# A bidirectional state-space layer on one core: gates by tanh without a clamp on POOL, softplus products two steps apart, five slots for the dt diagonals, first inputs in halves

## Chip, core and metric

The kernel runs on one core of a Trainium2 chip. The metric is the time of one execution on the device in microseconds (us). Engines go by their short names: PE is TensorE, DVE is VectorE, ACT is ScalarE, POOL is GpSimd, SP is SyncE (here it only starts DMAs). Each engine works through its own queue in order; a wait for a semaphore stops that engine's whole queue.

## What is computed

For 16 sequences of 256 tokens with 256 channels, in float32, a conditioned layer is computed: normalise and modulate, run a selective state-space model forward and backward, add, then a gated two-layer perceptron. Cut to the part that the change touches:

```python
xs, z = split(h @ in_w, 2)                   # 512 channels each
xs = silu(xs)
proj = xs @ xproj_w                          # dt, B, C
dt = softplus(proj[..., :512] + dt_bias)
hst = hst * exp(dt * A) + (dt * xs) * B      # 64 states per channel, one token after the other
y = sum(hst * C) + xs * Dskip
return y * silu(z) @ out_w                   # also backward over the tokens
```

Silu is x * sigmoid(x). Softplus is log(1 + exp(v)).

## The kernel before, in words

`main_phase` does everything up to `y`; `output_phase` does the rest and isn't touched. `main_phase` is unrolled completely. It makes 16 passes: 8 pairs of sequences (`CB = 2`), each in two directions. A pass is 128 steps (`JP`), and a step is one scan on DVE (`scan`, L889): a 128 x 1024 `tensor_tensor_scan` over 32 tokens of a part of the states. 16 steps are a chunk of 32 tokens, so a pass has 8 chunks, numbered from 0. Two steps are a pair; POOL's loop runs over the 64 pairs of a pass.

One step needs from the others:

- PE (`step`): for step j it injects the inputs into the bank `u[j % 2]` (`inject`, L1031, 4 matmuls in 2 parts), computes the exponents of step j + 2 (`exponent`, L1044), and adds up outputs of earlier steps (`add_up`, L1063). It may start step j when scan j - 2 has ended, since `u` has two slots.
- ACT (`one_pass`): `put_carry` (L816) writes the carried state of step j into bank `u`, then `decay` (L797, L798) takes the exponentials for step j + 2, and every eighth step `read_y` (L809) empties the output bank.
- POOL (`one_pass`, pair i): `turn_dt` (L535) makes the diagonal tile `dd` for pair i + 2, `turn_u` (L544) makes `ud` for pair i + 1, `carry_in` (L570 and L575) makes the carried state of steps 2i and 2i + 1, from chunk 1 on. `spread_c` (L557) comes once a chunk in its third pair, `first_inputs` (L563) once a chunk in its seventh pair, for the chunk that follows.
- The scan of step j waits for the inject, for `decay` and, from chunk 1 on, for `put_carry`; every eighth one also for an `add_up`.

Beside this, each pass carries the preparation of the following pass, a "unit", cut into small pieces. Each engine has a generator `unit(q)`; PE and ACT take one piece after each step (slot j), POOL takes two per pair from its third pair on, one between `carry_in(2i)` and `turn_u(i + 1)`, one after `carry_in(2i + 1)`. So piece k of POOL lies beside step k + 4. The slots of a unit: 16 projections of x and z, one each third slot from 0 to 45 (`project_xz`, L942, 4 recorded matmuls each); 8 half-projections of dt and 2 of B and C, each over two slots, from 48, 51, 54, 57, 60, 63, 72, 75, 84 and 87 on (`project`, L950); transposes at 66, 69, 78, 90 and 98. With an odd q the next pair of sequences is also normalised (`variance`, `root`, `normalise`) and turned (slots 108 and 112); DVE then takes its statistics between scans 64 and 78. The last pass has no unit. The unit of pass 0 runs before the first scan, without anything beside it.

Before, a gate takes: `take_xz` (L658) copies the projection out of PSUM in two halves; POOL clamps it from below (L473); ACT makes exp, log of 1 + that, and exp again (L642, L645, L648), one slot apart; POOL multiplies (L479). A softplus of a 128-channel block takes: Relu and Abs out of PSUM on ACT (L668, L669), exp, 1 + exp, log and minus 1 (L675 to L682, semaphore `logged`), then four products or sums on POOL (`softplus`, L485, L488, L492, L497) in four pieces one after the other, then 8 free pieces.

All of exp, log, Copy, Relu, Abs and Identity are in the one table set that ACT loads at the start (L613). Three PSUM banks, `e`, are handed out in `share_banks` to exponents and to the unit's matmuls; PE waits before a bank for whoever reads it last.

`dd` and `ud` have four slots each (`NPR`), so `turn_dt` of pair i + 2 waits until scan 2i - 3 has ended:

```python
pool.wait_ge(scanned, scanned_to(p, 2 * (i - NPR) + 1))
```

Of the kernel before, what the change touches and what calls it, by code (L numbers as in the profile page):

```python
# [58 lines left out]
def main_phase(nc, x, cond, w_mod, b_mod, w_in, w_xp, dt_bias, a_log, mod, scr):  # L59
# [4 lines left out]
    with ctx:  # L64
# [9 lines left out]
        NDA, NPR, NM, NDT = 4, 4, 4, 3  # L74
# [17 lines left out]
        dd = sb("b_dd", [P, NPR, TT, TC])  # L92
# [19 lines left out]
        cl = sb("b_cl", [P, 2, T])  # L112
# [65 lines left out]
        chain = sem("b_chain")  # L178
# [22 lines left out]
        UT_SLOT = (66, 78, 90, 98)  # L201
        BC_SLOT, BT_SLOT = 54, 69
        TURN_SLOT = (108, 112)
# [78 lines left out]
        with nc.Block() as block:  # L282
# [163 lines left out]
            def _(pool):  # L446
# [20 lines left out]
                def clamp(q, i):  # L467
                    m = q * SILUS + i
                    src = xs[:, i, :] if i < JB else sd[:, i - JB, :]
                    pool.wait_ge(freed, first_job(q) + CB * i + CB)  # L470
                    if m >= 2:
                        pool.wait_ge(silu_made, m - 1)
                    nc.gpsimd.tensor_scalar(cl[:, i % 2, :], src, CLAMP, None, ALU.max).then_inc(clamped, 1)  # L473

                def times_sigmoid(q, i):
                    m = q * SILUS + i
                    dst = xs[:, i, :] if i < JB else sd[:, i - JB, :]
                    pool.wait_ge(chain, 3 * m + 3)
                    nc.gpsimd.tensor_tensor(dst, dst, cl[:, i % 2, :], ALU.mult).then_inc(silu_made, 1)  # L479

                def softplus(q, j):
# [11 lines left out]
                    yield  # L493
# [4 lines left out]
                    yield  # L498

                def unit(q):  # L500
                    for i in range(SILUS):
                        clamp(q, i)
# [27 lines left out]
                def turn_dt(p, i):  # L530
# [3 lines left out]
                    pool.wait_ge(scanned, scanned_to(p, 2 * (i - NPR) + 1))  # L534
                    nc.gpsimd.tensor_tensor(dd[:, i % NPR, :, :], dr[:, c % 2, v:v + 1, :].broadcast_to((P, TT, TC)),  # L535
# [24 lines left out]
                def first_inputs(p, c):  # L560
                    pool.wait_ge(f_loaded[c % 2], loaded_to(p, c, F_DMAS))
                    flat = u0[:, c % 2, :, :, :].rearrange("p k v d -> p (k v d)")
                    nc.gpsimd.tensor_tensor(flat, flat, b0[:, c % 2, :].broadcast_to((P, DI)), ALU.mult).then_inc(u0_made, 1)  # L563
                    pool.wait_ge(u0_made, p * (NCH - 1) + c)
# [19 lines left out]
                def one_pass(p, last, side):  # L584
                    for i in range(PAIRS):
# [9 lines left out]
                        if v == STEPS // 2 - 2 and c + 1 < NCH:  # L595
                            first_inputs(p, c + 1)
# [12 lines left out]
            def _(act):  # L609
# [27 lines left out]
                def sigmoid(q, i):  # L637

                    m = q * SILUS + i
                    both = cl[:, i % 2, :]  # L640
                    act.wait_ge(clamped, m + 1)
                    nc.scalar.activation(both, both, ACT.Exp, scale=-1.0).then_inc(chain, 1)  # L642
                    yield
                    act.wait_ge(chain, 3 * m + 1)
                    nc.scalar.activation(both, both, ACT.Ln, bias=1.0).then_inc(chain, 1)  # L645
                    yield
                    act.wait_ge(chain, 3 * m + 2)
                    nc.scalar.activation(both, both, ACT.Exp, scale=-1.0).then_inc(chain, 1)  # L648

                def take_xz(q, i, b):  # L650
                    n = first_job(q) + CB * i + b
                    act.wait_ge(full, n + 1)
# [5 lines left out]
                    nc.scalar.activation(dst[:, b * SEQ:(b + 1) * SEQ], job_bank(n)[:, 0:SEQ], ACT.Copy).then_inc(freed, 1)  # L658
# [52 lines left out]
                def unit(q):  # L711
                    for i in range(SILUS):
# [812 lines left out]
```

## Time and profile before

| | us |
|---|---|
| median of 3 runs | 5516.26 (5516.01 to 5521.09) |
| the profiled execution | 5517.54 |
| its span, first to last instruction | 5515.8 |
| mean granted PE clock | 0.974 |
| busy: PE, DVE, ACT, POOL | 5024.7, 4741.2, 3408.5, 3910.0 |
| DVE's scans (2048) | 4554.2 |
| first scan starts, last scan of the last pass ends | 118.9, 5057.9 |

The rows further down are of four kinds. The page's busy line and groups of instructions give totals. Windows give a stretch (from:to and its length), how much of it PE, the weight load PEld, DVE, ACT and POOL were busy (with the number of instructions), the granted PE clock as a share of full speed, the DMA share and GB/s. The timeline lists instructions in order of time: start, length, engine, line, operation, tiles, and in square brackets how long the engine sat idle and who ended it. Adjacent instructions of one engine overlap a little in the records: two scans that follow one another without a wait start 2.18 us apart, though one is recorded as 2.29 us. So a shown idle time of x stands for a delay of about x + 0.11. Rows of equal instructions without a wait between them are merged (x3).

### The profile page before, as it was taken

The page shows a single profiled execution, that of the slowest core. Times are in us where ns is not written, and L with a number is a line of the kernel's source. Part 1 is how long each engine was busy: PE and PEld are TensorE (multiplying, and loading weights), DVE is VectorE, ACT ScalarE, POOL GpSimd, SP SyncE. Part 2 cuts the span into 40 slices and gives each one's busy share as a digit, 9 for nine tenths or more (in the row PEclk, how much of TensorE's full clock was granted, in tenths as well). Part 3 has the DMA queues.
Part 4 walks back from the last instruction along what each step waited for, and adds up shares of the span by engine and source line. Part 5 has one row for each costly group of instructions (what it writes and reads, how often), then busy time and mean ns, then how long its engine had stood idle before and what let it go on. Part 6 is the DMA issues. An engine that isn't in the chain of part 4 may idle for free. (4 is left out here: it accounts for less than half of the span.)

```text
span 5515.8 us, 130520 instructions
## 1 busy us (share of the span) xinstructions
PE 5024.7 (91%) x44784; PEld 2544.5 (46%) x44784; DVE 4741.2 (86%) x2419; ACT 3408.5 (62%) x11450; POOL 3910.0 (71%) x6629
## 2 busy tenths in 40 slices
PE   5999989898999989898999989898999989886898
PEld 4444444444444444444544444444444444443444
DVE  1989898989989898989989898989989898997443
ACT  4766666666766666666766666666766666564111
POOL 4877777787877777787877777787877777674111
PEclk8999999999999999999999999999999999998999
DMA  3111111111111111111111111111111111112552
GB/s 101 50 49 49 56 34 61 42 50 48 52 50 49 54 36 60 42 51 48 51 50 49 54 36 57 45 52 48 51 50 44 53 37 45 35 29 82 156 156 65
DMA packets 433144, 306.75 MB, mean 56 GB/s; under 512 B 215920, under 2 KB 336240, under 8 KB 432496
## 3 DMA queue, kind: packets, MB, share of 16 engines
q1 hardware_dynamic: 428272, 294.39, 17.8%
q8 instruction: 349, 5.72, 0.4%
q10 hardware_dynamic: 4224, 4.19, 0.2%
q14 instruction: 299, 2.45, 0.1%
HBM read 187.27 MB, written 111.15 MB: 54 GB/s over the span
## 5 line engine op out<-in xcount | busy, mean ns | idle before, releaser
L889 DVE TENSOR_TENSOR_SCAN b_hs<-b_dA,b_u 128x1024 f32<-128x1024 f32 x2048 | 4554.2, 2272 | 394.0 <-ACT b_u L816 309.8
L1044 PE MATMUL b_ex<-b_dd,b_aw 32*128 32x512 f32 x8192 | 2794.6, 651 | 59.0 <-ACT b_dA L798 31.3
L1031 PE MATMUL b_u<-b_ud,b_bw 32*128 32x256 f32 x16384 | 2364.3, 405 | 314.0 <-DVE b_hs L889 305.3
L798 ACT ACTIVATE b_dA<-b_ex 128x496 f32<-128x496 f32 x4096 | 2290.5, 589 | 180.6 <-PE b_ex L1044 178.4
L1031 PEld LDWEIGHTS b_u<-b_ud,b_bw 32*128 32x128 f32 x16384 | 1456.0, 187 | 1200.7 <-issue 719.6
L535 POOL TENSOR_TENSOR b_dd<-b_dr,b_mask 128x512 f32<-128x512 f32 x1024 | 1072.5, 1047 | 567.2 <-DVE b_hs L889 546.6
L1063 PE MATMUL b_y<-b_hs,b_cw 128*32 128x256 f32 x16384 | 1329.7, 396 | 2.3 <-DVE b_hs L889 2.3
L816 ACT ACTIVATE b_u<-b_hin 128x32 f32<-128x32 f32 x1792 | 364.9, 204 | 1361.9 <-PE b_u L1031 868.2
L544 POOL TENSOR_TENSOR b_ud<-b_ur,b_mask 128x512 f32<-128x512 f32 x1024 | 1082.3, 1057 | 0.0
L1044 PEld LDWEIGHTS b_ex<-b_dd,b_aw 32*128 32x128 f32 x8192 | 874.6, 186 | 109.4 <-ACT b_dA L798 70.0
L1063 PEld LDWEIGHTS b_y<-b_hs,b_cw 128*32 128x32 f32 x16384 | 326.5, 109 | 1055.9 <-issue 1055.3
L797 ACT ACTIVATE b_first<-b_ex 128x16 f32<-128x16 f32 x3584 | 644.1, 180 | 13.0 <-PE b_ex L1044 7.3
L575 POOL TENSOR_TENSOR b_hin<-b_hm,b_u 128x32 f32<-128x32 f32 x1792 | 450.8, 252 | 140.4
L570 POOL TENSOR_TENSOR b_hm<-b_first,b_hs 128x32 f32<-128x32 f32 x1792 | 480.3, 268 | 94.2 <-ACT b_first L797 85.7
L950 PE MATMUL b_ex<-b_xs,b_wxp 128*128 128x256 f32 x1256 | 353.8, 405 | 0.7 <-ACT b_ey L669 0.7
L1199 POOL TENSOR_TENSOR c_gs<-c_gs,c_sz 128x512 f32<-128x512 f32 x64 | 79.0, 1274 | 302.1 <-DVE c_gs L1405 302.1
L942 PE MATMUL b_ex<-b_hT,b_win 128*128 128x256 f32 x1008 | 288.2, 410 | 5.3 <-ACT b_hT L628 3.1
L950 PEld LDWEIGHTS b_ex<-b_xs,b_wxp 128*128 128x128 f32 x1256 | 214.7, 190 | 142.4 <-issue 99.2
L942 PEld LDWEIGHTS b_ex<-b_hT,b_win 128*128 128x128 f32 x1008 | 174.4, 192 | 120.8 <-issue 96.9
L485 POOL TENSOR_TENSOR b_nd<-b_wy,b_ey 128x512 f32<-128x512 f32 x64 | 81.4, 1272 | 183.3 <-ACT b_wy L682 183.3
L473 POOL TENSOR_SCALAR b_cl<-b_xs 128x512 f32<-128x512 f32 x64 | 95.0, 1485 | 124.0 <-ACT b_xs L658 124.0
L473 POOL TENSOR_SCALAR b_cl<-b_sd 128x512 f32<-128x512 f32 x64 | 95.0, 1484 | 82.1 <-ACT b_sd L658 82.1
(106 smaller groups left out, 2491.2 us busy)
## 6 DMA issues: line engine op xcount, KB each, us to landing
b_u<-scratch_ut SPq DMA_DIRECT2D x256, 128.0 KB, 2.9
scratch_y<-b_ysb SPq DMA_DIRECT2D x128, 256.0 KB, 2.3
scratch_xs<-b_xs SPq DMA_DIRECT2D x64, 256.0 KB, 2.1
scratch_sz<-b_sd SPq DMA_DIRECT2D x64, 256.0 KB, 2.2
scratch_dt<-b_sd SPq DMA_DIRECT2D x64, 256.0 KB, 2.2
scratch_ut<-b_uT SPq DMA_DIRECT2D x64, 256.0 KB, 2.3
b_ur<-scratch_ut SPq DMA_DIRECT2D x1024, 16.0 KB
b_dr<-scratch_dt SPq DMA_DIRECT2D x1024, 16.0 KB, 1.7
```

The costliest lines, as they stand in the source:

```text
L535: nc.gpsimd.tensor_tensor(dd[:, i % NPR, :, :], dr[:, c % 2, v:v + 1, :].broadcast_to((P, TT, TC)), mask[:, :].unsqueeze(2).broadcast_to(( ...
L544: nc.gpsimd.tensor_tensor(ud[:, i % NPR, :, :, :], ur[:, c % 2, :, v * TT:(v + 1) * TT].unsqueeze(3).broadcast_to(shape), mask[:, :].unsqu ...
L570: nc.gpsimd.tensor_tensor(hm[:, j % NM, :, :].rearrange("p h d -> p (h d)"), e0[:, j % NM, :, :].rearrange("p h d -> p (h d)"), hs[:, v, : ...
L575: nc.gpsimd.tensor_tensor(hin[:, j % NM, :, :], hm[:, j % NM, :, :], u0[:, c % 2, 2 * kp:2 * kp + 2, v, :], ALU.add).then_inc(hin_made, 1)
L797: nc.scalar.activation(e0[:, j % NM, h, :], src[:, :, 0], ACT.Exp).then_inc(e0_done, 1)
L798: nc.scalar.activation(dA[:, j % NDA, h, :, 1:TC], src[:, :, 1:TC], ACT.Exp).then_inc(exp_done, 1)
L889: nc.vector.tensor_tensor_scan(hs[:, v, :, :, kp].rearrange("p d t -> p (d t)"), dA[:, j % NDA, :, :, :].rearrange("p h d t -> p (h d t)") ...
L942: last = nc.tensor.matmul(job_bank(n)[:, 0:SEQ], win[:, k, i * P:(i + 1) * P], hT[:, q % DIRS, k, b * SEQ:(b + 1) * SEQ], start=(k == 0), ...
L950: ins = nc.tensor.matmul(job_bank(n)[:, 0:SEQ], wxp[:, k, cols], xs[:, k, b * SEQ:(b + 1) * SEQ], start=(k == 0), stop=(k == JB - 1))
L1031: ins = nc.tensor.matmul(dst[:, :, tb, :], bw[row(r), c % 2, tb, :], ud[row(r), j // 2 % NPR, tb, :, :], start=(tb == 0), stop=(tb == NTB ...
L1044: nc.tensor.matmul(e[bank_of[what]][:, :], aw[row(r), p % DIRS, v, :, :].rearrange("p b s -> p (b s)"), dd[row(r), j // 2 % NPR, :, :].rea ...
L1063: ins = nc.tensor.matmul(y[q * QR:(q + 1) * QR, cols], cw[:, n, q, g * QR:(g + 1) * QR], hs[:, f * (SPN // 2):(f + 1) * (SPN // 2), :, q * ...
```

## The change

- A gate becomes x/2 * (1 + tanh(x/2)). `take_xz` reads PSUM twice, once with Copy and scale 0.5, once with Tanh and scale 0.5 into `th`; `plus_one` adds 1 on ACT one slot after the second half; POOL multiplies as before. The clamp on POOL and the three functions on ACT are gone. Before Tanh, ACT waits until POOL's product of two gates earlier is done (`silu_made`).
- Tanh is in another table set. Each unit loads `exp_and_others` at its start and `natural_log_exp_and_others` after the gates (slot 48).
- The four pieces of `softplus` on POOL stand two pieces apart, with 4 free pieces behind them and not 8. What hangs on the last of them moves: the fourth transpose from slot 98 to 101, ACT's root from 101 to 103, the turning from 108 and 112 to 110 and 114.
- `dd` has five slots, with a running index over passes, so `turn_dt` of pair i + 2 waits for scan 2i - 5.
- `first_inputs` is done in two halves, in the sixth and the seventh pair of a chunk.

```diff
-        NDA, NPR, NM, NDT = 4, 4, 4, 3
+        NDA, NPR, NDD, NM, NDT = 4, 4, 5, 4, 3
...
-        UT_SLOT = (66, 78, 90, 98)
+        UT_SLOT = (66, 78, 90, 101)
         BC_SLOT, BT_SLOT = 54, 69
-        TURN_SLOT = (108, 112)
+        TURN_SLOT = (110, 114)
...
-                def clamp(q, i):
-                    m = q * SILUS + i
-                    src = xs[:, i, :] if i < JB else sd[:, i - JB, :]
-                    pool.wait_ge(freed, first_job(q) + CB * i + CB)
-                    if m >= 2:
-                        pool.wait_ge(silu_made, m - 1)
-                    nc.gpsimd.tensor_scalar(cl[:, i % 2, :], src, CLAMP, None, ALU.max).then_inc(clamped, 1)
-
                 def times_sigmoid(q, i):
...
-                    pool.wait_ge(chain, 3 * m + 3)
-                    nc.gpsimd.tensor_tensor(dst, dst, cl[:, i % 2, :], ALU.mult).then_inc(silu_made, 1)
+                    pool.wait_ge(raised, m + 1)
+                    nc.gpsimd.tensor_tensor(dst, dst, th[:, i % 2, :], ALU.mult).then_inc(silu_made, 1)
...
                     nc.gpsimd.tensor_tensor(nd[:, :], wy[:, :], ey[:, :], ALU.subtract).then_inc(nd_made, 1)
-                    yield
+                    yield from wait_steps(2)
...
                 def unit(q):
                     for i in range(SILUS):
-                        clamp(q, i)
                         yield from wait_steps(2)
...
                         yield from softplus(q, j)
                         if j < JB - 1:
-                            yield from wait_steps(8)
+                            yield from wait_steps(4)
                     if q % DIRS and q + 1 < PASSES:
                         c = q // DIRS + 1
-                        yield from wait_steps(2)
                         variance(c)
...
-                    pool.wait_ge(scanned, scanned_to(p, 2 * (i - NPR) + 1))
-                    nc.gpsimd.tensor_tensor(dd[:, i % NPR, :, :], dr[:, c % 2, v:v + 1, :].broadcast_to((P, TT, TC)),
+                    pool.wait_ge(scanned, scanned_to(p, 2 * (i - NDD) + 1))
+                    nc.gpsimd.tensor_tensor(dd[:, (p * PAIRS + i) % NDD, :, :], dr[:, c % 2, v:v + 1, :].broadcast_to((P, TT, TC)),
...
-                def first_inputs(p, c):
+                def first_inputs(p, c, k):
                     pool.wait_ge(f_loaded[c % 2], loaded_to(p, c, F_DMAS))
...
+                    some = u0[:, c % 2, 2 * k:2 * k + 2, :, :].rearrange("p k v d -> p (k v d)")
+                    nc.gpsimd.tensor_tensor(some, some, b0[:, c % 2, :].broadcast_to((P, DI // 2)), ALU.mult).then_inc(u0_made, 1)
+                    if k:
+                        pool.wait_ge(u0_made, 2 * (p * (NCH - 1) + c))
...
-                        if v == STEPS // 2 - 2 and c + 1 < NCH:
-                            first_inputs(p, c + 1)
+                        if v in (STEPS // 2 - 3, STEPS // 2 - 2) and c + 1 < NCH:
+                            first_inputs(p, c + 1, v - (STEPS // 2 - 3))
...
-                    nc.scalar.activation(dst[:, b * SEQ:(b + 1) * SEQ], job_bank(n)[:, 0:SEQ], ACT.Copy).then_inc(freed, 1)
+                    nc.scalar.activation(dst[:, cols], job_bank(n)[:, 0:SEQ], ACT.Copy, scale=0.5)
+                    if m >= 2:
+                        act.wait_ge(silu_made, m - 1)
+                    nc.scalar.activation(th[:, i % 2, cols], job_bank(n)[:, 0:SEQ], ACT.Tanh, scale=0.5).then_inc(freed, 1)
+
+                def plus_one(q, i):
+                    act.wait_ge(freed, first_job(q) + CB * i + CB)
+                    nc.scalar.activation(th[:, i % 2, :], th[:, i % 2, :], ACT.Identity, bias=1.0).then_inc(raised, 1)
...
                 def unit(q):
+                    nc.scalar.preload_act_table_set("exp_and_others")
                     for i in range(SILUS):
                         take_xz(q, i, 0)
...
                         take_xz(q, i, 1)
                         yield
-                        next(last, None)
-                        yield
-                        yield
-                    last = sigmoid(q, SILUS - 1)
-                    next(last)
+                        plus_one(q, i)
+                        yield from wait_steps(2)
+                    nc.scalar.preload_act_table_set("natural_log_exp_and_others")
```

## Rows read from the trace of the kernel before

**Rows 1.** The page, part 1: busy us (share of the span) xinstructions.

```profile
PE 5024.7 (91%) x44784; PEld 2544.5 (46%) x44784; DVE 4741.2 (86%) x2419; ACT 3408.5 (62%) x11450; POOL 3910.0 (71%) x6629
```

**Rows 2.** Windows: pass 4, steps 0-47, 48-97, 98-127; last pass, steps 0-47.

```profile
1363.68:1474.17 110.49, 106.02 (x1025) 53.74 (x1025) 106.52 (x50) 78.43 (x249) 88.41 (x137) 1.00 0.16 49
1474.17:1605.84 131.67, 126.72 (x1099) 63.94 (x1099) 114.26 (x58) 86.39 (x305) 102.28 (x181) 0.97 0.19 55
1605.84:1675.67 69.83, 60.01 (x614) 28.89 (x613) 65.98 (x32) 45.00 (x163) 50.98 (x95) 1.00 0.12 33
4779.00:4883.53 104.53, 83.89 (x960) 42.77 (x960) 104.53 (x49) 61.58 (x210) 69.99 (x125) 1.00 0.11 28
```

**Rows 3.** Waits, whole span: who waited for whom, us in total, times, longest.

```profile
POOL b_dd L535 <- DVE b_hs L889: 546.6, 441, 7.2
POOL b_nd L485 <- ACT b_wy L682: 183.3, 64, 3.8
```

**Rows 4.** Timeline of POOL, pass 4, steps 56 to 58: the first softplus.

```profile
1494.57 1.27 POOL L485 TENSOR_TENSOR b_nd<-b_wy,b_ey 128x512 f32<-128x512 f32 x1 [3.63 <-ACT b_wy L682]
1495.80 1.05 POOL L544 TENSOR_TENSOR b_ud<-b_ur,b_mask 128x512 f32<-128x512 f32 x1
1496.82 0.26 POOL L570 TENSOR_TENSOR b_hm<-b_first,b_hs 128x32 f32<-128x32 f32 x1
...
1497.37 1.27 POOL L488 TENSOR_TENSOR b_nd<-b_ln,b_nd 128x512 f32<-128x512 f32 x1
```

**Rows 5.** Timeline of DVE, pass 4: scans 49, 56, 57, 81, 89, 93 and 96.

```profile
1476.68 2.29 DVE L889 TENSOR_TENSOR_SCAN b_hs<-b_dA,b_u 128x1024 f32<-128x1024 f32 x1 [0.23 <-ACT b_u L816]
...
1494.74 2.29 DVE L889 TENSOR_TENSOR_SCAN b_hs<-b_dA,b_u 128x1024 f32<-128x1024 f32 x1 [0.63 <-PE b_y L1063]
1497.77 2.29 DVE L889 TENSOR_TENSOR_SCAN b_hs<-b_dA,b_u 128x1024 f32<-128x1024 f32 x1 [0.75 <-ACT b_u L816]
...
1560.42 2.29 DVE L889 TENSOR_TENSOR_SCAN b_hs<-b_dA,b_u 128x1024 f32<-128x1024 f32 x1 [0.77 <-ACT b_u L816]
...
1581.75 9.00 DVE L889 TENSOR_TENSOR_SCAN b_hs<-b_dA,b_u 128x1024 f32<-128x1024 f32 x4 [0.23 <-ACT b_u L816]
1592.63 2.29 DVE L889 TENSOR_TENSOR_SCAN b_hs<-b_dA,b_u 128x1024 f32<-128x1024 f32 x1 [1.89 <-ACT b_u L816]
...
1601.46 6.64 DVE L889 TENSOR_TENSOR_SCAN b_hs<-b_dA,b_u 128x1024 f32<-128x1024 f32 x3 [0.76 <-PE b_y L1063]
```

**Rows 6.** Timeline of PE, pass 4: step 49's inject, its half-projection, step 50's inject.

```profile
1475.01 0.48 PE L1031 MATMUL b_u<-b_ud,b_bw 32*128 32x256 f32 x2
...
1476.67 1.13 PE L950 MATMUL b_ex<-b_xs,b_wxp 128*128 128x256 f32 x4
1477.73 0.48 PE L1031 MATMUL b_u<-b_ud,b_bw 32*128 32x256 f32 x2
```

**Rows 7.** Timelines of POOL and DVE, pass 4, steps 28 and 29: a clamp, then all first inputs.

```profile
1425.57 1.49 POOL L473 TENSOR_SCALAR b_cl<-b_sd 128x512 f32<-128x512 f32 x1 [1.60 <-ACT b_sd L658]
...
1428.03 1.04 POOL L563 TENSOR_TENSOR b_u<-b_u,b_b 128x512 f32<-128x512 f32 x1
...
1430.11 4.46 DVE L889 TENSOR_TENSOR_SCAN b_hs<-b_dA,b_u 128x1024 f32<-128x1024 f32 x2 [1.16 <-ACT b_u L816]
```

**Rows 8.** Groups by line: busy us, mean ns of one | idle before.

```profile
L563 POOL TENSOR_TENSOR b_u<-b_u,b_b 128x512 f32<-128x512 f32 x112 | 116.5, 1040 | 0.0
L1345 ACT ACT_TABLE_LOAD x8 | 10.3, 1283 | 0.1
```

**Rows 9.** Timeline of ACT, pass 4, step 48 into step 49.

```profile
1474.77 0.67 ACT L642 ACTIVATE b_cl<-b_cl 128x512 f32<-128x512 f32 x1
1476.35 0.20 ACT L816 ACTIVATE b_u<-b_hin 128x32 f32<-128x32 f32 x1 [0.91 <-PE b_u L1031]
```

**Rows 10.** Timeline of POOL before the first scan: two clamps, one gate apart.

```profile
44.69 1.48 POOL L473 TENSOR_SCALAR b_cl<-b_xs 128x512 f32<-128x512 f32 x1 [0.45 <-ACT b_xs L658]
47.86 1.48 POOL L473 TENSOR_SCALAR b_cl<-b_sd 128x512 f32<-128x512 f32 x1 [0.45 <-ACT b_sd L658]
```

More of the change, by code:

```diff
@@ L492, in softplus @@
                     nc.gpsimd.tensor_tensor(sd[:, j, :], pre[:, :], nd[:, :], ALU.add).then_inc(dt_made, 1)
-                    yield
+                    yield from wait_steps(2)
                     pool.wait_ge(dt_made, m + 1)
@@ L497, in softplus @@
                     nc.gpsimd.tensor_tensor(us[:, j % 2, :], sd[:, j, :], xs[:, j, :], ALU.mult).then_inc(u_made, 1)
-                    yield
+                    yield from wait_steps(2)
                 def unit(q):
                     for i in range(SILUS):
-                        clamp(q, i)
                         yield from wait_steps(2)
@@ L635, in modulate, with take_xz @@
                     yield
-                def sigmoid(q, i):
+                def take_xz(q, i, b):
                     m = q * SILUS + i
[L640 to L650, printed above, removed]
                     n = first_job(q) + CB * i + b
+                    cols = slice(b * SEQ, (b + 1) * SEQ)
                     act.wait_ge(full, n + 1)
@@ L711, in unit @@
                 def unit(q):
+                    nc.scalar.preload_act_table_set("exp_and_others")
                     for i in range(SILUS):
                         take_xz(q, i, 0)
-                        last = sigmoid(q, i - 1) if i else wait_steps(2)
-                        yield
-                        next(last, None)
-                        yield
-                        next(last, None)
-                        yield
+                        yield from wait_steps(3)
                         take_xz(q, i, 1)
                         yield
-                        next(last, None)
-                        yield
-                        yield
-                    last = sigmoid(q, SILUS - 1)
-                    next(last)
+                        plus_one(q, i)
+                        yield from wait_steps(2)
+                    nc.scalar.preload_act_table_set("natural_log_exp_and_others")
                     for j in range(JB):
@@ L729, in unit @@
                         take_dt(q, j, 0)
-                        next(last, None)
-                        yield
-                        yield
-                        next(last, None)
-                        yield
+                        yield from wait_steps(3)
                         take_dt(q, j, 1)
@@ L763, in unit @@
                             next(logs, None)
-                            yield from wait_steps(7)
+                            yield from wait_steps(10)
                     take_ut(q, 3)
@@ L767, in unit @@
                         c = q // DIRS + 1
-                        yield from wait_steps(3)
+                        yield from wait_steps(2)
                         root(c)
@@ L1006, in unit @@
                             turn_inputs(q, 2)
-                            yield from wait_steps(8)
+                            yield from wait_steps(11)
                     turn_inputs(q, 3)
                     if q % DIRS and q + 1 < PASSES:
-                        yield from wait_steps(10)
+                        yield from wait_steps(9)
                         for k in range(MB):
@@ L1044, in exponent @@
                     nc.tensor.matmul(e[bank_of[what]][:, :], aw[row(r), p % DIRS, v, :, :].rearrange("p b s -> p (b s)"),
-                                     dd[row(r), j // 2 % NPR, :, :].rearrange("p d t -> p (d t)"),
+                                     dd[row(r), (p * PAIRS + j // 2) % NDD, :, :].rearrange("p d t -> p (d t)"),
                                      start=True, stop=True, tile_position=(r * QR, 0), skip_group_check=True
```

9 lines of the change are left out of this document (3 added, 6 removed).

## The prediction

> **What bounds the kernel now.** I read the busy line first [rows 1]. PE is at 91% and DVE at 86%, so neither is simply the bound, and POOL at 71% looks harmless. The windows say more [rows 2]. In the last pass, which carries no unit, 48 scans take 104.53 us, 2.178 us each, DVE has no gap, and PE is busy for 80% of it: that is the floor of the main phase. In pass 4 the same 48 steps take 110.49 us, 5.96 more; these are the steps with the gates. The next 50 steps, with softplus, take 131.67 us against 50 x 2.178 = 108.9, 22.8 more. The last 30 take 69.83 against 65.3, 4.5 more. So a pass with a unit pays some 33 us for it, with an odd q; about 30 without normalising. Over 15 passes that is nearly 480 us, all that this change can touch, apart from the time before the first scan.
>
> Who makes DVE late? For softplus the POOL timeline shows it [rows 4]. POOL waits 3.63 us for the log. Then it makes the first product (next start 1.23 later), and only then `ud` (1.02) and the carried state (0.55), which scan 57 needs; it starts late by 0.75 + 0.11 = 0.86 [rows 5]. From then on POOL is behind, and each step has one softplus piece, one diagonal tile and one carry: 1497.37 - 1494.57 = 2.80 us against 2.18 of a scan. So each of the next three steps is 0.62 late too. POOL idles 183.3 us in all before such a first product and 546.6 us before `dd` [rows 3], yet delays DVE: its work comes in bursts.
>
> PE is the second cause. A half-projection makes its step 1477.73 - 1475.01 = 2.72 us [rows 6], 0.54 over a scan, and there are two in a row. The stretch from scan 48 (1474.17, where the window of rows 2 starts) to scan 56 (1494.74, rows 5) holds three such doubles and no softplus piece on POOL: 20.57 us for 8 scans, 3.15 over, so 1.05 per double. The change doesn't touch this. A single projection costs 2.72 + 1.67 (from inject to scan, rows 5 and 6) - 2 x 2.178 = 0.03, plus about 0.15 of hand-over: 0.2.
>
> **The gates (steps 0 to 47).** The clamp of 1.49 leaves POOL, 8 per pass. Its place was bad: it waits for ACT (1.60), stands before `ud` and the carry, and in step 28 first inputs of 1.04 follow it, so scan 29 is 1.16 + 0.11 late [rows 7]. What is left for POOL is one product of 1.24 in 6 steps beside 2 x 1.57 per pair, 4.4 us in the fullest pair against 4.36. I take POOL's part as gone. What is late next is PE: ten single projections of 0.2, and at steps 16 and 40, where the scan also waits for an output sum behind a projection, 0.4 each (an estimate: the hand-over again, and scan 56 waits 0.63 for such a sum, rows 5): 2.9 with step 8. So 5.96 - 2.9 = **3.0 us per pass**. Ends: 1.5 (PE takes back what POOL gives) and 4.
>
> On ACT a gate loses three functions on 512 columns (0.67, rows 9) and gains two more halves and one function on 512. Tanh has no row here; I bound it by a third and by three times that 0.67, and take the same length as Exp, since all functions in the groups differ little. Net ACT has less to do, 0.5 us per gate, and at step 49 no log stands before the next carry any more: I count 0.3 us per pass. The new wait before Tanh stands in front of `put_carry` and `decay`. POOL's product of two gates earlier comes right after carry(6i), ACT's Tanh at the end of step 6i behind a projection, about 1.5 us after that carry is needed; the product takes 1.24. Cost nothing; if the cover goes, see the rivals.
>
> **Two table loads per pass.** A load is recorded as 1.283 us [rows 8]. The first falls in chunk 0, where ACT has no carry to write and decays two steps ahead: nothing. The second stands at step 48 in place of an exp that starts at 1474.77; ACT would be done at 1476.05, and it waits until 1476.35 for PE anyway [rows 9]. Nothing again; ends 0 and the whole 2.6 us per pass.
>
> The Trainium skill (ScalarE: Activation LUTs, What ACT_TABLE_LOAD costs) speaks against this: a switch costs the load and a drain of about 1.38 us, 2.66 in all. No row here shows a drain. By that rule the load at step 48 would end 1.1 us after PE released the carry, and the sum would be some 16 us worse over 15 passes.
>
> **Softplus two pieces apart (steps 48 to 97).** All four pieces now lie in one half of each pair, so a step with a piece (2.80) alternates with one without (1.57): 4.37 for two scans, 4.36. POOL no longer falls further behind, but it doesn't catch up either, and the first product still waits for the log and stands before the carry. So the first delay stays each time (57, 69, 81, 93), as does PE's part.
> - Scans 48 to 56: 3.15 stays.
> - From 56 to 81: 1560.42 - 1494.74 = 65.68, 11.2 over 25 scans' 54.45 [rows 5]. Left over: first delays 0.86 + 0.75 + 0.88, DVE's own statistics 0.7, four doubles of PE at 1.05 (the fifth is covered by the delay of 57), and 0.8 since halves of the first inputs meet pieces of softplus in pairs 29 and 30. That is 8.2, a gain of 3.0.
> - From 81 to 89: 21.33, 3.9 over. Two doubles of 1.05 stay: gain 1.8.
> - From 89 to 96: 19.71, 4.5 over. Scan 93 waits 1.89, because first product, `ud` and all first inputs (1.04) stand before its carry. With half of these it is some 0.4 better. Behind it, from 93 to 96, three scans take 8.83, 2.3 over: in this stretch the granted clock is 0.97 on average [rows 2], so for about 131.67 x 0.03 x 2 = 8 us PE ran at 1.2 GHz instead of 2.4, after it had stood behind that same late carry. I assume that it still falls, and take 1.05 for the stretch; if it doesn't, 1.3 more.
>
> Together 5.9; ends 3.5 (each delay that POOL gives up shows up as one of PE) and 12 (the first delays go too).
>
> **Five slots** let `dd` start a pair earlier, so more of the 546.6 us of waiting [rows 3] can be spent ahead. But `carry_in` follows in the same queue and waits for ACT's decay, and before each burst POOL idles already for the log. I count nothing; ends 0 and 2 us per pass. **Halved first inputs**: 1.04 [rows 8] becomes twice something between 0.52 and 1.04, counted above. They need their DMA 2 steps sooner; it has never been waited for (0.0, rows 8). SP's queue for chunk 7 moves back by up to 2 steps, behind the dt store; ends 0 and one scan per pass. **Shifted slots**: the dt store, the fourth transpose and the turning move by 2 or 3 of 128 slots with room behind them; the normalising now meets a half of first inputs: 0.3 us in 7 passes, a loss of 2.
>
> **Before the first scan** nothing covers the gates. They are 47.86 - 44.69 = 3.17 us apart [rows 10], 8 of them; POOL's clamp hands to three functions of ACT. Without it PE is the slowest, two projections of 1.06 (rows 6) each, 2.1. So 8 x 1.05 = **8.4 us**; ends 5 and 11.
>
> **The sum.** 15 x (3.0 + 5.9 + 0.3) = 138, minus 2, plus 8.4: 144.4. The profiled execution (5517.54) stands 1.3 over the median, so I take the difference from the median: 5516.3 - 144 = **5372 us**.
>
> **The rivals.**
> 1. *PE takes it back.* Each delay of POOL today gives PE time in which its doubles go unseen. For: the doubles lie on the same steps as the softplus pieces. By the lower ends, 15 x (1.5 + 3.5) + 5 = 80: about **5436**. Against: the stretch 81 to 89 has 0.62 late scans where no double stands. Chance 0.17.
> 2. *Only PE is left.* With a slot more and no clamp POOL gets ahead of the bursts, and the clock no longer falls. 15 x (4 + 12) + 11 = 251: about **5265**; halfway there, 5310. Against: the first product waits for ACT, not for POOL. Chance 0.15.
> 3. *The table switch costs more than its record.* The trace has no instruction hard behind a load, so it can hold ACT beyond 1.283 us. It decides from 1.58 on (1476.35 - 1474.77); with as much again, 1.283, it is 1.0 x 15 = 15 us: **5387**. Chance 0.15.
> 4. *Slower.* ACT stands before Tanh for POOL's product, and ACT's own decays, which POOL's next carry needs, stand behind it: a circle. It decides from where POOL reaches carry(6i) later than ACT's step 6i. Then each gate costs up to product and carry, 1.24 + 0.55, on DVE: 8 x 1.8 x 15 = 215 us, less the 144: about **5590**. Against: POOL has lost work just there and idled 1.6 us before the clamp. Chance 0.04.
> 5. *The main phase doesn't move*, since POOL's delays are all replaced: only the start gains, **5508**. Chance 0.03.
>
> The forecast has 0.46. From 5300 to 5440 lie the forecast, rival 3 and most of rivals 1 and 2. A measurement of this kernel can tell about 0.2% (11 us) from no change: faster 0.93, same 0.02, slower 0.05.
>
> **What would show it.** Right: no delay of 0.62 in scans 58 to 60, 70 to 72, 82 to 84; scan 29 on time; delays at 57, 69 and 81 as before, 93 near 1.5; doubles still 1.05; first scan at 110.5; ACT idle after the load at step 48. Wrong: ACT waiting for POOL before Tanh, low clock in new places, waits before the first halves, or doubles above 1.05.

## Result, and the profile after

The changed kernel takes 5384.93 us (median of 4 runs, 5378.22 to 5390.21); the kernel before, measured beside it, 5518.24. The ratio is 0.9757, with a 95% interval of 0.9741 to 0.9774: 133 us less, where 144 were forecast. The profiled execution took 5380.16 (span 5378.4, mean granted PE clock 0.981), 137.4 less in span than the one of before.

The page's busy line of after, to hold against [rows 1]:

```profile
PE 4902.5 (91%) x44784; PEld 2509.1 (47%) x44784; DVE 4725.0 (88%) x2419; ACT 3391.5 (63%) x11482; POOL 3758.3 (70%) x6613
```

It looks like the one before. POOL lost 152 us of work and ACT 17, yet PE, which runs as many instructions as before, shows 122 us less too. A part of it is the clock: in the main phase the granted clock stood at half for 160 us before and for 101 after, which makes up some 30 of the 122. The rest is not explained here. The windows of pass 4 (steps 0 to 47, 48 to 97, 98 to 127, with columns as in [rows 2]) say where it went:

```profile
1322.45:1430.33 107.88, 104.23 (x1025) 54.07 (x1025) 105.99 (x49) 76.86 (x251) 77.77 (x134) 1.00 0.16 50
1430.33:1556.01 125.68, 119.86 (x1096) 61.02 (x1095) 113.67 (x60) 86.80 (x305) 99.10 (x176) 0.99 0.19 57
1556.01:1627.69 71.68, 61.12 (x613) 29.32 (x614) 66.11 (x31) 45.21 (x163) 55.06 (x103) 0.98 0.13 35
```

The gates take 2.6 us less, softplus 6.0 less, and the end of the pass 1.9 **more**. One pass is a sample. So here is a table of my own over all passes, from the ends of the 2048 scans: for each stretch, how much longer its scans took than 2.178 us each, per pass, as means over 7 passes with normalising (numbers 0, 2, to 12) and 7 without (1, 3, to 13).

| steps | before, with / without | after, with / without |
|---|---|---|
| 0-47 | 6.25 / 6.40 | 3.82 / 3.65 |
| 48-56 | 3.30 / 3.29 | 3.08 / 3.12 |
| 57-80 | 10.39 / 10.98 | 9.28 / 8.45 |
| 81-88 | 4.49 / 4.53 | 2.64 / 2.65 |
| 89-96 | 4.82 / 5.13 | 3.38 / 2.70 |
| 97-127 | 4.45 / 0.02 | 5.64 / 0.03 |
| sum | 33.7 / 30.4 | 27.8 / 20.6 |

First scan at 108.9 us against 118.9; main phase (first scan to last scan's end) 4820.1 against 4939.0; the rest, code that the change doesn't touch, 449.4 against 458.0. So 10.0 + 118.9 = 128.9 of the 137.4 lie where the change is, and 8.6 in the output phase, which varied from 449 to 461 between the kernels of this study and belongs to no edit.

**The first softplus**, pass 4, on POOL, as in [rows 4]:

```profile
1450.64 1.27 POOL L477 TENSOR_TENSOR b_nd<-b_wy,b_ey 128x512 f32<-128x512 f32 x1 [4.66 <-ACT b_wy L669]
1451.87 1.07 POOL L534 TENSOR_TENSOR b_ud<-b_ur,b_mask 128x512 f32<-128x512 f32 x1
1452.88 0.27 POOL L561 TENSOR_TENSOR b_hm<-b_first,b_hs 128x32 f32<-128x32 f32 x1
1453.24 0.25 POOL L566 TENSOR_TENSOR b_hin<-b_hm,b_u 128x32 f32<-128x32 f32 x1
1453.44 1.05 POOL L525 TENSOR_TENSOR b_dd<-b_dr,b_mask 128x512 f32<-128x512 f32 x1
...
1455.00 1.28 POOL L480 TENSOR_TENSOR b_nd<-b_ln,b_nd 128x512 f32<-128x512 f32 x1
```

After the carry for step 57 `dd` follows at once, and the second product starts only 3.1 us after the first has ended (1.5 before). DVE in pass 4 from scan 56 on, then scans 81 and 93 and the end of the pass, as in [rows 5]:

```profile
1450.81 2.29 DVE L866 TENSOR_TENSOR_SCAN b_hs<-b_dA,b_u 128x1024 f32<-128x1024 f32 x1 [0.62 <-PE b_y L1040]
1453.85 4.46 DVE L866 TENSOR_TENSOR_SCAN b_hs<-b_dA,b_u 128x1024 f32<-128x1024 f32 x2 [0.75 <-ACT b_u L793]
1459.25 4.46 DVE L866 TENSOR_TENSOR_SCAN b_hs<-b_dA,b_u 128x1024 f32<-128x1024 f32 x2 [0.93 <-ACT b_u L793]
...
1514.90 8.86 DVE L866 TENSOR_TENSOR_SCAN b_hs<-b_dA,b_u 128x1024 f32<-128x1024 f32 x4 [0.78 <-ACT b_u L793]
...
1544.89 28.63 DVE L866 TENSOR_TENSOR_SCAN b_hs<-b_dA,b_u 128x1024 f32<-128x1024 f32 x13 [1.47 <-ACT b_u L793]
1573.91 2.29 DVE L866 TENSOR_TENSOR_SCAN b_hs<-b_dA,b_u 128x1024 f32<-128x1024 f32 x1 [0.40 <-ACT b_u L793]
1577.63 11.34 DVE L866 TENSOR_TENSOR_SCAN b_hs<-b_dA,b_u 128x1024 f32<-128x1024 f32 x5 [1.43 <-ACT b_u L793]
1591.20 9.00 DVE L866 TENSOR_TENSOR_SCAN b_hs<-b_dA,b_u 128x1024 f32<-128x1024 f32 x4 [2.23 <-PE b_y L1040]
1601.53 28.42 DVE L866 TENSOR_TENSOR_SCAN b_hs<-b_dA,b_u 128x1024 f32<-128x1024 f32 x13 [1.33 <-ACT b_u L793]
```

Scan 57 still waits 0.75, scan 58 now follows without a wait, 60 too. Scan 59 waits 0.93: it is a double of PE, which the delay of 57 used to hide in part. In the last lines scans 107, 112 and 116 wait 1.43, 2.23 and 1.33; in the kernel before the same stretch had two such waits, 1.14 and 1.32.

**The table load** at slot 48 on ACT, and scan 49:

```profile
1430.91 0.47 ACT L786 ACTIVATE b_ysb<-b_y 128x128 f32<-128x128 f32 x2
1431.40 1.28 ACT L707 ACT_TABLE_LOAD   x1
1432.69 0.20 ACT L793 ACTIVATE b_u<-b_hin 128x32 f32<-128x32 f32 x1
```

```profile
1433.03 2.29 DVE L866 TENSOR_TENSOR_SCAN b_hs<-b_dA,b_u 128x1024 f32<-128x1024 f32 x1 [0.43 <-ACT b_u L793]
```

The load starts 1.07 us after scan 48 does (1430.33), behind `read_y`; the exp of before started 0.60 after it. It ends 2.36 after it, and before ACT wrote this carry 2.18 after it [rows 2, 9]. So scan 49 is 0.2 later than before. The carry starts at the end of the load's record: no drain shows. From a load's start to ACT's next instruction it is 1.29 us in 31 of the 32 loads of units; behind the very first one, before the first scan, ACT also waits 0.93 us for PE.

### The profile page after: what moved, and what is told of

It is laid out like the page before. It is cut to its first block and busy times, and to the rows that moved or that the text cites. A ratio compares the mean times of both kernels' runs of the same rounds, so it can differ in the third digit from the quotient of the medians.

```text
span 5378.4 us, 130410 instructions
## 1 busy us (share of the span) xinstructions
PE 4902.5 (91%) x44784; PEld 2509.1 (47%) x44784; DVE 4725.0 (88%) x2419; ACT 3391.5 (63%) x11482; POOL 3758.3 (70%) x6613
## 5 line engine op out<-in xcount | busy, mean ns | idle before, releaser
L1021 PE MATMUL b_ex<-b_dd,b_aw 32*128 32x512 f32 x8192 | 2688.8, 648 | 50.2 <-ACT b_dA L775 21.8
L525 POOL TENSOR_TENSOR b_dd<-b_dr,b_mask 128x512 f32<-128x512 f32 x1024 | 1074.9, 1050 | 224.5 <-DVE b_hs L866 209.6
L561 POOL TENSOR_TENSOR b_hm<-b_first,b_hs 128x32 f32<-128x32 f32 x1792 | 483.6, 270 | 573.7 <-ACT b_first L774 550.7
L1021 PEld LDWEIGHTS b_ex<-b_dd,b_aw 32*128 32x128 f32 x8192 | 834.9, 185 | 90.5 <-ACT b_dA L775 52.9
L553 POOL TENSOR_TENSOR b_u<-b_u,b_b 128x256 f32<-128x256 f32 x224 | 138.0, 616 | 7.5 <-DMA b_u<-scratch_ut 7.2
L786 ACT ACTIVATE b_ysb<-b_y 128x128 f32<-128x128 f32 x512 | 119.8, 305 | 6.3 <-PE b_y L1040 6.3
```

What stands on the lines that cost most here:

```text
L525: nc.gpsimd.tensor_tensor(dd[:, (p * PAIRS + i) % NDD, :, :], dr[:, c % 2, v:v + 1, :].broadcast_to((P, TT, TC)), mask[:, :].unsqueeze(2). ...
L561: nc.gpsimd.tensor_tensor(hm[:, j % NM, :, :].rearrange("p h d -> p (h d)"), e0[:, j % NM, :, :].rearrange("p h d -> p (h d)"), hs[:, v, : ...
L1021: nc.tensor.matmul(e[bank_of[what]][:, :], aw[row(r), p % DIRS, v, :, :].rearrange("p b s -> p (b s)"), dd[row(r), (p * PAIRS + j // 2) % ...
```

## Experiments

Each kernel is the changed one with one edit. Ratios are to the kernel before, on the same chip. "Undone" means that part as it was before.

### The spacing of softplus undone

```diff
-                    yield from wait_steps(2)
+                    yield
...
-                            yield from wait_steps(4)
+                            yield from wait_steps(8)
```

(The first edit stands behind each of the four pieces; the normalising keeps its place.)

> The changed kernel with the four softplus pieces of POOL in a row again (8 free pieces behind them); all else as changed. Theory of the prediction: each block's second to fourth piece makes a scan 0.62 us late again, three per block, four blocks, less what PE's doubles hide: some 5 us per pass, 75 us in all, about 5460 us, with delays near 0.6 at scans 58 to 60, 70 to 72, 82 to 84. Rival (PE takes it back): PE's doubles lie on the same steps, so under 2 us per pass, below 5415 us.

Measured: 5474.28 us, ratio 0.9915 (0.9898 to 0.9931), 89 us over the changed kernel. Main phase 4909.2. DVE, scans 57 to 60 of pass 4:

```profile
1476.86 2.29 DVE L867 TENSOR_TENSOR_SCAN b_hs<-b_dA,b_u 128x1024 f32<-128x1024 f32 x1 [0.74 <-ACT b_u L794]
1479.64 2.29 DVE L867 TENSOR_TENSOR_SCAN b_hs<-b_dA,b_u 128x1024 f32<-128x1024 f32 x1 [0.50 <-ACT b_u L794]
1483.02 2.29 DVE L867 TENSOR_TENSOR_SCAN b_hs<-b_dA,b_u 128x1024 f32<-128x1024 f32 x1 [1.08 <-ACT b_u L794]
1485.80 4.54 DVE L867 TENSOR_TENSOR_SCAN b_hs<-b_dA,b_u 128x1024 f32<-128x1024 f32 x2 [0.50 <-ACT b_u L794]
```

The row of late scans is back (0.50 + 0.11, the 0.62 of before; at scan 59 a double of PE comes on top). By the table's measure a pass loses 5.5 (with) to 6.4 us (without normalising). PE does not take the gain back.

### The gates undone

```diff
-                    nc.scalar.activation(th[:, i % 2, cols], job_bank(n)[:, 0:SEQ], ACT.Tanh, scale=0.5).then_inc(freed, 1)
...
+                    nc.gpsimd.tensor_scalar(cl[:, i % 2, :], src, CLAMP, None, ALU.max).then_inc(clamped, 1)
```

(The other lines of the gates, table loads included, are reversed with them.)

> The changed kernel with the gates of before (clamp on POOL, three functions on ACT, one table set); all else as changed. Theory of the prediction: 3.3 us per pass (50 us) and about 10 us before the first scan: about 5445 us; the first scan starts near 119 us again and scan 29 is late. Rival (with a fifth slot and halved first inputs POOL hides the clamp by itself): only the start is lost, about 5395 us.

Measured: 5437.77 us, ratio 0.9853 (0.9836 to 0.9869), 53 us over the changed kernel, where 60 were expected. First scan at 119.1; steps 16 to 47 pay 5.5 us per pass against 3.15 to 3.3. Steps 0 to 47 as a whole pay 2.0 to 2.1 more than in the changed kernel, not the 2.4 to 2.8 that the table shows between before and after. With the clamp and the first inputs in halves, scans 29 and 31 are late by 0.85 and 0.49 (passes without normalising), in the kernel before by 1.27 and 0.94. So beside a clamp the halves seem to be worth something; without it, in these steps, whole first inputs cost nothing (below). In the changed kernel the products of two gates before the first scan are 1.76 us apart, on POOL:

```profile
42.19 1.27 POOL L471 TENSOR_TENSOR b_xs<-b_xs,b_th 128x512 f32<-128x512 f32 x1 [0.49 <-ACT b_th L645]
43.95 1.27 POOL L471 TENSOR_TENSOR b_sd<-b_sd,b_th 128x512 f32<-128x512 f32 x1 [0.48 <-ACT b_th L645]
```

It was 3.17 in [rows 10]. This product waits for ACT's "plus one".

### Four slots for dd

```diff
-        NDA, NPR, NDD, NM, NDT = 4, 4, 5, 4, 3
+        NDA, NPR, NDD, NM, NDT = 4, 4, 4, 4, 3
```

> The changed kernel with four slots for dd; all else as changed. Theory of the prediction: the slot is worth nothing by itself, since POOL idles for the log before each burst anyway: within 10 us of the changed kernel, 5380 to 5395 us. Rival (the slot lets POOL get ahead of its bursts, so it carries part of the gain): 2 us per pass, about 5415 us.

Measured: 5385.62 us, ratio 0.9758 (0.9742 to 0.9774): the fifth slot is worth nothing. POOL's waits (us in total, times, longest), of after and then of this kernel, show why:

```profile
POOL b_hm L561 <- ACT b_first L774: 550.7, 711, 3.3
POOL b_dd L525 <- DVE b_hs L866: 209.6, 111, 3.6
```

```profile
POOL b_dd L525 <- DVE b_hs L866: 779.7, 649, 6.8
POOL b_hm L561 <- ACT b_first L774: 74.5, 112, 1.7
```

With a slot more, POOL spends its idle time one instruction later, before the carry, for ACT.

### First inputs in one piece

```diff
-                        if v in (STEPS // 2 - 3, STEPS // 2 - 2) and c + 1 < NCH:
-                            first_inputs(p, c + 1, v - (STEPS // 2 - 3))
+                        if v == STEPS // 2 - 2 and c + 1 < NCH:
+                            first_inputs(p, c + 1)
```

> The changed kernel with the first inputs in one product in the seventh pair of a chunk; all else as changed. Theory of the prediction: scan 93 is later by 0.4 us and perhaps the clock stays low longer behind it, 0.5 to 1 us per pass lost: about 5395 us. Rival: at the end of passes with an odd q the halves meet the normalising and wait for their DMA (scan 107 is 1.5 us late in the changed kernel), so that whole first inputs gain about 1 us there in 7 passes: between 5378 and 5385 us, no change.

Measured: 5388.25 us, ratio 0.9766 (0.9749 to 0.9783), which can't be told from the changed kernel. Steps 89 to 96 pay 0.65 more, and steps 57 to 80 and 97 to 127 together 0.4 to 0.7 less. A half costs 0.62 us, so two cost 1.23 instead of 1.04, and their loads are now waited for:

```profile
L553 POOL TENSOR_TENSOR b_u<-b_u,b_b 128x256 f32<-128x256 f32 x224 | 138.0, 616 | 7.5 <-DMA b_u<-scratch_ut 7.2
```

### The softplus pieces in the other half of the pair

The changed kernel's first product stands before `ud` and the carry that a scan is about to need. One slot later it stands behind this carry, before `dd`.

```diff
                     times_sigmoid(q, SILUS - 1)
-                    yield from wait_steps(3)
+                    yield from wait_steps(4)
...
                         variance(c)
-                        yield from wait_steps(4)
+                        yield from wait_steps(3)
```

(The second edit keeps the normalising in its place.)

> The changed kernel with all softplus pieces of POOL one piece later (53, 55, 57, 59 and so on): the first product then stands behind carry(57) and in front of carry(58), so it no longer delays the carry that is due when the log ends; POOL waits for the same log. Theory: the first delays (0.86 at 57, 0.76 at 69, 0.89 at 81, 1.57 at 93) go, and with 93 the low clock behind it; the double projection at slot 57, which the delay covered, shows up again with 0.5 to 1. Gain 2.5 to 4 us per pass, 40 to 60 us: about 5335 us. Rival (PE takes it back everywhere): under 1 us per pass, above 5370 us.

Measured: 5281.78 us, ratio 0.9567 (0.9551 to 0.9583): 103 us **under** the changed kernel, about twice what was expected. POOL, pass 4, the first product:

```profile
1422.31 1.27 POOL L477 TENSOR_TENSOR b_nd<-b_wy,b_ey 128x512 f32<-128x512 f32 x1 [1.55 <-ACT b_wy L669]
1423.54 1.05 POOL L525 TENSOR_TENSOR b_dd<-b_dr,b_mask 128x512 f32<-128x512 f32 x1
1424.55 0.27 POOL L561 TENSOR_TENSOR b_hm<-b_first,b_hs 128x32 f32<-128x32 f32 x1
```

and DVE, scans 56 to 58:

```profile
1422.48 4.46 DVE L866 TENSOR_TENSOR_SCAN b_hs<-b_dA,b_u 128x1024 f32<-128x1024 f32 x2 [0.63 <-PE b_y L1040]
1427.30 2.29 DVE L866 TENSOR_TENSOR_SCAN b_hs<-b_dA,b_u 128x1024 f32<-128x1024 f32 x1 [0.35 <-ACT b_u L793]
```

The carry of scan 57 has gone by before POOL waits for the log, and scan 57 follows scan 56 without a wait. The product takes nothing from DVE any more: what stays at scan 58 is PE's double. The late scans 57, 69, 81 and 93 alone made up 4.2 to 4.6 us of a pass; all four are on time now. Per pass, with / without normalising: 57 to 80 pay 6.13 / 5.32 instead of 9.28 / 8.45, 81 to 88 1.52 instead of 2.65, 89 to 96 0.56 / 0.52 instead of 3.38 / 2.70. The mean granted clock rises from 0.981 to 0.988, and of the low-clock stretches near scans 69 and 93 none is left. So the 6.4 to 6.8 us that a pass gains are the late carries and the clock behind them together; no run parts the two.

### Turning later

The normalising pieces two slots apart, the turning at 113 and 117 instead of 110 and 114.

```diff
-        TURN_SLOT = (110, 114)
+        TURN_SLOT = (113, 117)
...
                             normalise(c, t)
-                            yield
+                            yield from wait_steps(2)
```

(with ACT's and PE's own waits before the turning 3 slots longer.)

> The changed kernel with POOL's four normalising pieces two apart (they were in a row) and the turning at slots 113 and 117 instead of 110 and 114, so that ACT's two modulating blocks don't delay step 112, whose scan also waits for an output sum. Only the 7 passes with an odd unit can gain. Theory: scans 106 to 108 (2.3 us late) come on time, and step 112's delay shrinks to that of a plain step: 2.5 to 3 us in 7 passes, 20 us: about 5365 us. Rival (the end of those passes is bound by ACT's modulating wherever it stands): under 1 us per such pass, 5378 to 5385 us.

Measured: 5374.49 us, ratio 0.9734 (0.9717 to 0.975), 10 under the changed kernel, half of what was expected. The intervals of the two ratios overlap, so the total alone doesn't settle it; the stretch does. Steps 97 to 127 pay 3.82 instead of 5.64 in the 7 passes; that is 13 us, and the delay is now under that before the change (4.45).

### Both moves together

The two diffs above in one kernel.

> Both edits of the two runs before this one on the changed kernel. They lie in different steps, so the gains should add up: 60 to 80 us, about 5315 us, faster than both kernels. Rival: above 5350 us.

Measured: 5272.69 us (5271.32 to 5274.29), ratio 0.955 (0.9534 to 0.9566), 112 under the changed kernel and the fastest of the study. Its windows for pass 4, cut at the same steps:

```profile
1292.74:1400.63 107.89, 104.23 (x1025) 54.07 (x1025) 106.00 (x49) 76.77 (x251) 77.59 (x134) 1.00 0.16 50
1400.63:1520.75 120.12, 113.75 (x1096) 59.48 (x1095) 112.93 (x59) 86.46 (x305) 99.54 (x179) 1.00 0.19 59
1520.75:1589.89 69.14, 58.68 (x613) 28.48 (x614) 65.99 (x31) 44.93 (x163) 54.46 (x100) 1.00 0.14 36
```

The softplus stretch takes 120.12 us, 11.5 less than in [rows 2], and the granted clock is 1.00 in all three windows. A pass still pays 19.2 or 14.2 us.

### Half of each half-projection

```diff
-                    for k in range(JB):
+                    for k in range(2):
```

(`stop`, and the point between the two slots, move with it: two slots with one matmul each. The output is another.)

> The changed kernel with half of the matmuls of the dt, B and C projections left out (rows 256 to 511 of xproj_w aren't used, so the output is another): a half-projection adds 0.53 us to its step on PE and not 1.06, and the step stays within a scan. Theory: the doubles cost 1.05 us each because PE's step is 2.72 us; halved they cost nothing, except where POOL's first delays stand: 6.5 to 9 us per pass less, 5245 to 5290 us. Rival (the delays of steps 48 to 97 come from ACT's or POOL's work, and PE's records only look full): under 3 us per pass less, above 5335 us.

Measured: 5321.8 us in a single run, 63 under the changed kernel, 4.2 per pass (5.1 with, 3.2 without normalising). Steps 48 to 55, with three doubles and no piece of softplus, pay 1.2 instead of 2.4: with half the matmuls a double's delay is halved, not gone. Steps 66 to 80 gain only 0.8 to 1.1. The gain lies between the theory's range and the rival's, and fits neither. Where PE is on time, carries that wait for POOL remain or come forward (in pass 4 those of scans 57, 59, 61, 69, 74, 81, 85 and 93). And PE is not always on time: scans 71 and 72 of pass 4 are late by 1.37 and 1.10, more than the 0.75 and 0.15 of the changed kernel, in a stretch at 1.2 GHz behind scan 69. DVE, scans 57 to 60 of pass 4:

```profile
1434.45 4.46 DVE L866 TENSOR_TENSOR_SCAN b_hs<-b_dA,b_u 128x1024 f32<-128x1024 f32 x2 [0.51 <-ACT b_u L793]
1439.41 4.46 DVE L866 TENSOR_TENSOR_SCAN b_hs<-b_dA,b_u 128x1024 f32<-128x1024 f32 x2 [0.50 <-ACT b_u L793]
```

Scans 57 and 59 wait 0.51 and 0.50 instead of 0.75 and 0.93.

### Two more table loads at slot 48

```diff
+                    nc.scalar.preload_act_table_set("exp_and_others")
+                    nc.scalar.preload_act_table_set("natural_log_exp_and_others")
```

> The changed kernel with three table loads in a row at slot 48 of each unit and not one (two more per unit, 16 units, of which 15 stand beside scans). If a load holds ACT for its recorded 1.28 us, step 49's scan is 2.6 us later in each of 15 passes, as little of it is still hidden: 30 to 40 us, about 5420 us. By the Trainium skill (ScalarE: Activation LUTs, What ACT_TABLE_LOAD costs) each switch costs 2.66 us with its drain; then it would be 80 us, about 5465 us. If the loads run beside other work of ACT: no change, 5385 us.

Measured: 5443.72 us, ratio 0.9874 (0.9845 to 0.9902), 59 us over the changed kernel (65 by the two ratios; only two executions): 3.9 per pass for two loads. ACT, pass 4:

```profile
1447.85 1.28 ACT L707 ACT_TABLE_LOAD   x1
1449.14 1.28 ACT L708 ACT_TABLE_LOAD   x1
1450.43 1.28 ACT L709 ACT_TABLE_LOAD   x1
1451.72 0.20 ACT L795 ACTIVATE b_u<-b_hin 128x32 f32<-128x32 f32 x1
```

Three loads hold ACT for 3.87 us, 1.29 each: there is no drain between them or behind them. The two added ones hold it for 2.57, 39 us over 15 passes, as expected of the record alone. The rest shows on PE. Windows of the same kernel, one ahead of scan 49's start and two behind it:

```profile
1448.60:1452.05 3.45, 2.37 (x20) 1.14 (x16) 0.44 (x1) 3.43 (x6) 0.38 (x1) 1.00 0.24 43
1452.05:1455.50 3.45, 2.95 (x12) 1.21 (x16) 2.64 (x2) 2.40 (x9) 1.52 (x3) 0.56 0.12 27
1455.50:1459.00 3.50, 3.50 (x28) 1.41 (x20) 2.21 (x2) 1.25 (x6) 1.93 (x5) 0.50 0.10 25
```

PE has been busy for 2.37 of 3.45 us, since it stood for ACT; then the granted clock falls from 1.00 to 0.50 (1.2 GHz), and with two half-projections due PE is busy for all of the last window: scans 50 and 51 wait 0.81 and 1.29, against 0.17 and none in the changed kernel. Steps 48 to 55 pay 6.3 to 7.1 us instead of 2.4. The passes themselves part the two costs. In 4 of the 15 (0, 9, 10 and 14) the clock stays up behind scan 49, and steps 48 to 56 pay 2.3 to 2.5 more than in the changed kernel; in the 11 where it falls they pay 3.8 to 5.7 more. At 2.3 each that is 35 us for the loads and 28 for the clock; further on the passes differ both ways, 2 us less in all.

## Why the prediction held, and where not

**Gates, 3.0 + 0.3 forecast, 2.6 measured** (table, steps 0 to 47), with 0.2 more in 48 to 56. By the run with the gates undone 2.0 to 2.1 of the 2.6 are the gates' own; the other 0.3 to 0.8 came with the other edits, most likely the halved first inputs, which was not tested beside a clamp. POOL's part is gone: in steps 0 to 47 no carry is late for it, and scan 29, late by 1.27 in [rows 7], follows without a wait (read from pass 4). What is left are PE's single projections, 0.15 to 0.4 in twelve steps (2.9 had been counted, about 3.2 stay). What I had at nothing was the first table load: in steps 0 to 15 a pass pays 0.2 to 0.3 more, of which 0.19 stands at scan 4, beside the load at slot 0. The second load was to leave ACT idle before the next carry; it ends 0.2 behind that moment. My start for it was that of the exp [rows 9], 0.47 us too early.

**The price of a table load.** Wherever ACT waits for nothing else, the next instruction starts 1.29 us after the load does, so the record is the whole price on ACT, and the 16 us by the rule (the Trainium skill, ScalarE: Activation LUTs, What ACT_TABLE_LOAD costs) are not there. Rival 3, that a load holds ACT beyond its record, falls by the same numbers. But the two added loads showed that a price on one engine is no upper end of what it costs: steps 48 to 56 lost some 28 us on top of the 35, in passes where PE's clock fell.

**Softplus, 5.9 forecast, 4.4 with normalising and 6.8 without** (steps 57 to 96; the 0.2 in 48 to 56 is counted with the gates). The mean of the two fits and the terms don't: the stretch from 57 to 80 gained less than forecast and that from 89 to 96 more. That they nearly cancel is luck.
- 48 to 56: 3.15 was to stay; about 3.1 did, where the table has 3.3 before.
- 57 to 80: 3.0 forecast, 1.1 and 2.5 measured. The three delays of 0.62 are gone in each of the three first blocks, and those of 57, 69 and 81 have stayed, as forecast (0.75 to 0.78 plus 0.11). But I had counted four doubles as in the open and the fifth, at 59, as covered by 57's delay. It isn't: scan 59 waits 0.93 + 0.11. And a stretch at 1.2 GHz from scan 69 or 70 on, in 2 passes with normalising and 5 of the others before, now stands in 5 and 2 of them; that goes the way of the difference between 1.1 and 2.5, which no run shows by itself.
- 81 to 88: 1.8 forecast, 1.85 and 1.88 measured. Two doubles are left.
- 89 to 96: 1.05 forecast, 1.4 and 2.4 measured. Scan 93 is 1.58 late, as forecast (1.5). I had assumed the clock to fall behind it as before. Before it fell there in all 15 passes, for 6.8 us; now in 11, and in 9 of these for 3.4.

**End of the pass, a loss of 0.3 forecast, 1.2 measured.** The term, which stands in the seven normalising passes, was mis-sized fourfold, for two reasons. On POOL a normalising piece, `ud` and a half of the first inputs stand between the carries of steps 106 and 107, and scan 107 is 1.54 late (1.18 in the other six):

```profile
1573.53 1.22 POOL L464 TENSOR_SCALAR b_xn<-b_xn,b_mv,b_rstd 128x256 f32<-128x256 f32 x1
1574.72 1.06 POOL L534 TENSOR_TENSOR b_ud<-b_ur,b_mask 128x512 f32<-128x512 f32 x1
1575.74 0.62 POOL L553 TENSOR_TENSOR b_u<-b_u,b_b 128x256 f32<-128x256 f32 x1
```

And the turning moved by 2 slots "with room behind": with TURN_SLOT at 110 ACT's two Identity halves (1.05) fall in step 111, so that PE waits 1.02 us for the bank, and scan 112 waits for an output sum besides. Here is PE, then ACT, pass 4 of after:

```profile
1588.65 0.69 PE L1021 MATMUL b_ex<-b_dd,b_aw 32*128 32x512 f32 x1 [1.02 <-ACT b_hT L619]
```

```profile
1587.55 1.05 ACT L619 ACTIVATE b_hT<-b_ex,mod 128x256 f32<-128x256 f32 x2
```

Pass 4, whose windows show 1.9 more, is one of two passes in which the clock also falls here (scan 112 is late by 2.34 and 2.13 in them, by 1.64 to 1.87 in the other five). A step that is moved must be held against what its new neighbours wait for in the same step, not only against free slots. Spacing both gave back 1.8.

**The parts that cost nothing.** Five slots: 0 forecast, 0 measured, for the reason given (the carry behind `dd` waits for ACT). Halved first inputs: within what can be told, with 7.2 us of waits for their loads in 6 places that I had at zero. **The start**: 8.4 forecast, 10.0 measured; the gates are 1.76 apart and not 2.1. I took PE as the slowest, at two projections of 1.06, but in a row PE starts one each 0.86 us (three take 2.75), and ACT, which works without idle from 38.51 to the last gate, sets the pace. The last gate's product starts 12.3 us sooner (49.22 against 61.49); 2.2 of that are lost again before the first softplus product (54.82 against 64.94), where the second table load stands uncovered, another term that I had at nothing. With two loads more the first scan starts 2.3 us later (111.2).

**The signs.** Of those for "right", the delays of 0.62, scan 29, and the delays at 57, 69, 81 and 93 came as listed; ACT was not idle after the load at step 48. Of those for "wrong", two were seen, both small: waits before the first halves (7.2 us), and low clock in new places, from scan 5 of pass 0 and from scan 111 of passes 4 and 8, 3.4 us each.

**The rivals.** 1 (PE takes it back) falls: undoing the spacing costs 89 us, and the doubles in the open have not grown. 4 (ACT stands for POOL's product before Tanh) falls: the waits of after have no such line. 5 falls with the main phase's 118.9 us. 2 named the next step. I argued against it that the first product waits for ACT and not for POOL, and that is so for this change; but the wait only costs DVE because a carry stands behind it in the same queue. One slot on, it costs nothing, and then POOL is clear of the bursts and the clock stays up: 5282, close to the 5265 of that rival. (Halfway from the forecast to it is 5319, not 5310.)

**Do the parts add up?** Undone one at a time, they cost 89 + 53 + 1 + 3 = 146 us against 133 for all together. The excess of 13 can't be told from nothing: each of the ratios has an interval of some 9 us to either side.

**What stays open.** Why the clock falls in one pass and not in the next at the same scan, with PE as busy ahead of it (last section). And in 57 to 80 about 6 us per pass are left in the best kernel; half the projections point to PE's doubles, but with POOL's part gone that was not measured.

## What to carry to other kernels

In an in-order queue the place of an instruction that waits is worth more than its length: put it right behind the last thing that someone needs soon, not before it; here one slot was worth 103 of 5385 us, more than each of the two larger edits. Spread side work so that each pair of steps holds no more than an engine's slack in it (here 4.36 - 2 x 1.57 = 1.2 us of POOL per pair), and when an edit moves a slot, list what else is due in the new step on every engine. A late hand-over can cost more than itself, by the clock of the engine that stood for it: here that was seen behind scan 49, late by 3.1 us, in 11 of 15 passes, and behind scan 93, late by 1.6, in as many.

## What the runs showed of the hardware

- ACT_TABLE_LOAD: 1.28 us recorded, 1.29 to the next instruction, alone or three in a row; no drain. It starts 0.02 us after the instruction before it has ended, where other neighbours on ACT overlap.
- PE's granted clock: 2.37 busy of 3.45 us ahead of a fall to 1.2 GHz; before, ahead of scan 93's stretch, 2.07 of 3.42. What PE did just before does not tell by itself. In the changed kernel it is busy for the same time around scan 93 in passes 6 and 4; in pass 6 the clock falls 0.93 us after the scan's start, in pass 4 it stays at 1.00. Pass 6, the same windows of pass 4 below it:

```profile
2149.13:2152.55 3.42, 2.48 (x20) 1.21 (x20) 1.95 (x2) 1.20 (x5) 3.26 (x6) 1.00 0.00 0
2152.55:2159.40 6.85, 6.85 (x42) 2.86 (x40) 5.57 (x3) 2.89 (x11) 6.62 (x10) 0.50 0.01 4
1542.34:1545.76 3.42, 2.49 (x20) 1.21 (x20) 1.95 (x2) 1.20 (x5) 3.26 (x6) 1.00 0.00 0
1545.76:1552.60 6.84, 5.99 (x62) 2.65 (x60) 6.79 (x4) 4.43 (x18) 6.61 (x11) 1.00 0.01 2
```

- A POOL product of 128 x 256 with a broadcast operand takes 0.616 us where 128 x 512 takes 1.04: halves cost 19% more in all.
- Freed time on POOL does not show as less waiting: with a fifth slot 550.7 us stand before the carry and 209.6 before `dd`; without it, 74.5 and 779.7.
